# A decoder's first self-attention on one core: projections ahead of all stack loads, three split buffers, and weight loads moved into the main steps

## The reference, cut to what matters

```python
qkv = x @ w_in.T + b_in
q, k, v = jnp.split(qkv, 3, axis=-1)                    # 16 heads of 16 features
scores = jnp.einsum('bhqd,bhkd->bhqk', q * scale, k) + causal_bias
attn = jax.nn.softmax(scores, axis=-1)
out = jnp.einsum('bhqk,bhkd->bhqd', attn, v).transpose(0, 2, 1, 3).reshape(...) @ w_out.T + b_out
x = _layernorm(x + out)
```

## Time and profile before

| what | value |
|---|---|
| median of three runs | 2646.59 us (2644.69 to 2653.12) |
| the profiled execution's own time | 2647.83 us |
| its span, first to last instruction | 2646.0 us |
| mean granted TensorE clock | 0.918 of full speed |
| PE, DVE, ACT, POOL busy | 80%, 55%, 47%, 25% of the span |
| DMA moved | 139.78 MB, mean 53 GB/s |

### The profile page before, as it was taken

One profiled execution on the slowest core, in us unless ns is written; L12 is line 12 of the kernel. 1 busy time (PEld: TensorE's weight loads), 2 busy tenths in 40 slices (PEclk: granted clock), 3 DMA queues, 4 the chain that ended last, 5 costly groups with the idle time before them and its releaser, 6 DMA issues. The chain is left out here.

```text
span 2646.0 us, 32547 instructions
## 1 busy us (share of the span) xinstructions
PE 2120.5 (80%) x11571; PEld 1193.6 (45%) x11586; DVE 1460.5 (55%) x2643; ACT 1243.4 (47%) x2672; POOL 674.2 (25%) x750
## 2 busy tenths in 40 slices
PE   3688888888888689999999533989899756787786
PEld 1234344344342455565555412556566532444444
DVE  3545366366563276766667368476662233556555
ACT  1154544544535265555555173757522223374662
POOL 4610320220010100000000257464340231432222
PEclk7799999999999899999999756999999967898898
DMA  6422433432321100000000100000000254533311
GB/s 162 120 58 67 88 70 72 84 74 57 67 49 37 59 19 7 19 15 19 17 7 11 62 26 0 27 16 25 11 27 13 89 98 97 117 84 85 68 52 41
DMA packets 127859, 139.78 MB, mean 53 GB/s; under 512 B 35933, under 2 KB 102369, under 8 KB 127602
## 3 DMA queue, kind: packets, MB, share of 16 engines
q1 hardware_dynamic: 127698, 137.69, 22.5%
HBM read 99.16 MB, written 38.47 MB: 52 GB/s over the span
## 5 line engine op out<-in xcount | busy, mean ns | idle before, releaser
L512 ACT ACTIVATE pbuf_sb<-psB 128x512 f32<-128x512 f32 (+1 forms) x608 | 330.7, 573 | 323.2 <-PE psB L394 300.5
L679 DVE TENSOR_REDUCE negm_sb<-psA 128x1 f32<-128x768 f32 (+6 forms) x352 | 346.9, 1022 | 159.1 <-PE psA L382 156.6
L1036 ACT ACTIVATE pw_sb<-psA,nmx_sb 128x154 f32<-128x154 f32 x512 | 192.0, 387 | 194.4 <-DVE nmx_sb L1127 194.4
L391 PE MATMUL psB<-qst_sb,kst_sb 99*128 99x512 bf16 (+3 forms) x768 | 232.3, 332 | 42.9 <-ACT pbuf_sb L512 34.7
L380 PE MATMUL psA<-kst_sb,qst_sb 96*128 96x512 bf16 (+3 forms) x768 | 198.2, 337 | 28.5 <-DVE negm_sb L679 25.4
L1127 DVE TENSOR_REDUCE nmx_sb<-psA 128x4 f32<-128x616 f32 x128 | 102.3, 799 | 176.4 <-PE psA L904 176.4
L408 PE MATMUL psO<-pbuf_sb,V_sb 128*32 128x512 f32 (+3 forms) x1536 | 168.0, 510 | 8.7 <-ACT OT_sb L498 7.4
L2481 DVE TENSOR_REDUCE negm_sb<-psA 128x4 f32<-128x640 f32 x128 | 104.0, 812 | 126.8 <-PE psA L2153 126.7
L2308 ACT ACTIVATE pb_sb<-psB 128x512 f32<-128x512 f32 x160 | 92.2, 598 | 150.3 <-PE psB L2163 149.9
L391 PEld LDWEIGHTS psB<-qst_sb,kst_sb 99*128 99x128 bf16 x768 | 74.3, 98 | 179.7 <-ACT pbuf_sb L512 146.3
L1076 POOL TENSOR_SCALAR std_sb<-mv_sb 128x1 f32<-128x1 f32 x32 | 7.3, 228 | 503.4 <-DVE mv_sb L1154 503.4
(11 more groups left out here) (267 smaller groups left out, 4550.1 us busy)
## 6 DMA issues: line engine op xcount, KB each, us to landing
qst_sb<-parts_dram SPq DMA_DIRECT2D x192, 128.0 KB, 4.4
rden_sb<-dens_dram SPq DMA_DIRECT2D x128, 128.0 KB, 2.7
parts_dram<-parts_sb SPq DMA_DIRECT2D x32, 384.0 KB, 2.5
kst_sb<-parts_dram SPq DMA_DIRECT2D x96, 128.0 KB, 7.1
x_dram<-X_sb SPq DMA_DIRECT2D x64, 128.0 KB, 1.7
parts_dram<-partsb_sb SPq DMA_DIRECT2D x16, 384.0 KB, 2.8
xT_sb<-xT SPq DMA_DIRECT2D x4, 1024.0 KB, 5.4
X_sb<-x SPq DMA_DIRECT2D x4, 1024.0 KB, 5.3
```

The source lines that it names most:

```text
L391: last = nc.tensor.matmul(psB[:, k, at:at + hi - lo], kst[0:MAX_ROWS, gg % 3, h, i * P:(i + 1) * P], qst[0:MAX_ROWS, gg % 3, h, lo:hi], st ...
L512: nc.scalar.activation(pbuf[:, key % 2, heads[0]:heads[-1] + 1, lo:hi], psB[:, (nb.n - 1) % 2, 0:len(heads) * (hi - lo)] .rearrange("p (h ...
L679: nc.vector.tensor_reduce(out=negm[:, gg % 2, heads[0]:heads[-1] + 1, j], in_=psA[:, (na.n - 1) % 2, :].rearrange("p (h n) -> p h n", h=le ...
L1036: last = nc.scalar.activation(pw[:, m % 2, h, :], psA[:, m % 2, at:at + K], ACT.Exp, bias=nmx[:, m % 2, h:h + 1], accum_out=psx[:, m % 3, ...
```

## The change: what it does, and the diff

- **Prologue loads.** The bias of q and k is loaded first, with a semaphore of its own; PE waits for wqkv (and xT0) alone. The raw feed-forward weights are no longer loaded here.
- **Three buffers of `q32`.** ACT may run one unit further ahead of the split.
- **SP's order.** Store units 0 to 4, stack 0, store units 5 to 7, then the main steps: xT0 of batch 1 and stack 1 at k = 0, `first_weights` (output projection, raw weights, `ones_dram`) at k = 1, stack 2 at k = 3, `late_weights` (13 DMAs) at k = 31.
- **Raw weights** are loaded into the room of `wk_x0` and `wv_x0`, which hold cross-attention weights later; so those are loaded only once the quantised weights are made. DVE sums them at k = 9 and 10, PE adds up at k = 12, POOL quantises in six steps at k = 18, 20, ..., 28. ACT no longer waits for them at k = 10.
- **Constants.** POOL fills only the columns of V that need ones, and the rows of `kst` one stack at a time: two before its eight `rest_of`, the third after.
- **Fourth stage.** Two bias rows (128 KB each when broadcast) are loaded there and not in the first stage.

```diff
-    q32 = sb("q32", [P, 2, 512], F32, first_stage)
+    q32 = sb("q32", [P, 3, 512], F32, first_stage)
-    w_raw = OT[:, 0:4, :].rearrange("p (i a) n -> p i (a n)", i=2)
+    ones = rden[:, 0:P]
+    w_raw1, w_raw2 = wk_x0[:, :, :], wv_x0[:, :, :].rearrange("p c n -> p (c n)")
+    W_AT = 12
 # SP
+            sp.dma_start(bqk_a0[:, :], t["L0_attn_b_inC"][:, 0:4]).then_inc(bqk_loaded, 16)
             sp.dma_start(wqkv[:, :, :], feature_rows(t["L0_attn_w_inT"])).then_inc(first_loaded, 16)
             sp.dma_start(xT0[:, :, :], ...).then_inc(xt_loaded, 16)
+            sp.dma_start(bv_a0[:, :], ...).then_inc(bv_loaded, 16)
...
-            for u in range(4):
+            for u in range(5):
                 store_parts(0, u)
             parts_landed(4)
             load_stack(0)
-            load_stack(1)
-            for u in range(4, 8):
+            for u in range(5, 8):
                 store_parts(0, u)
-            parts_landed(8)
-            load_stack(2)
+            def first_weights():
+                sp.wait_ge(wo_zeroed, 1)
+                ...                                     # wo_a0 (4 DMAs), bo_a0
+                sp.dma_start(w_raw1, feature_rows(t["L0_ffn_w1T"])).then_inc(raw_loaded, 16)
+                sp.dma_start(w_raw2..., feature_rows(t["L0_ffn_w2T"])).then_inc(raw_loaded, 16)
+                sp.wait_ge(consts_made, 3)
+                sp.dma_start(ones_dram, kst[QK_ROWS:QK_ROWS + 1, 0, 0, :]).then_inc(ones_stored, 16)
+            def late_weights():
+                sp.wait_ge(quantised, 2)
+                ...                                     # wk_x0, wv_x0, wq_x0 and ten small ones
             for k in range(LAST + 1):
                 if k < UNITS and kk == 0 and b + 1 < B:
                     ...                                 # xT0 of the next batch
+                if k == 0:
+                    load_stack(1)
+                if k == 1:
+                    first_weights()
+                if k == 3:
+                    parts_landed(8)
+                    load_stack(2)
+                if k == 31:
+                    late_weights()
                 if k >= 1 and qk_unit(k - 1):
                     store_parts(*qk_unit(k - 1))
 # PE
-            pe.wait_ge(first_loaded, 16 * 3)
+            pe.wait_ge(first_loaded, 16)
...
-            pe.wait_ge(summed, 2)
             pe.wait_ge(consts_made, 1)
+                if k == W_AT:
+                    pe.wait_ge(summed, 2)
+                    a = slot_a()
+                    nc.tensor.matmul(psA[:, a, 0:2], ones[:, :], asum[:, :], start=True, stop=True).then_inc(a_full, 1)
 # ACT, store_qk
-                if at >= 2:
-                    act.wait_ge(split_made, at - 1)
+                if at >= 3:
+                    act.wait_ge(split_made, at - 2)
-                    if s == 0:
-                        act.wait_ge(quantised, 2)
 # POOL
-            nc.gpsimd.memset(V[:, :, :, :], 1.0).then_inc(v_cleared, 1)
+            ...                                         # two fills of 256 elements a partition each
-            nc.gpsimd.memset(kst[QK_ROWS:MAX_ROWS, :, :, :], 1.0).then_inc(consts_made, 1)
-            for u in range(8):
-                rest_of(u)
+            for i in range(3):
+                nc.gpsimd.memset(kst[QK_ROWS:MAX_ROWS, i, :, :], 1.0).then_inc(consts_made, 1)
+                pool.wait_ge(consts_made, i + 1)
+                if i == 1:
+                    for u in range(8):
+                        rest_of(u)
+                if 18 <= k < 30 and k % 2 == 0:
+                    quantise((k - 18) // 2)
 # DVE
-            dve.wait_ge(first_loaded, 16 * 3)
+            dve.wait_ge(bqk_loaded, 16)
+                    if k in (W_AT - 3, W_AT - 2):
+                        sum_weights(k - W_AT + 3)
+                    if k == W_AT:
+                        weight_scales()
 # fourth stage, SP
             sp.dma_start(wkv_x1[:, :, :], feature_rows(t["L1_xattn_Wkv"])).then_inc(kv_loaded, 16)
+            sp.dma_start(bv_x1[:, :], ...).then_inc(kv_loaded, 16)
+            sp.dma_start(bo_x1[:, :], ...).then_inc(bo_loaded, 16)
```

More of the change, by code:

```diff
@@ L213, in a_slots @@
     def a_slots(k):
-        return NT + 1 + sum((len(first_units(query_tile(i))) + (i % 8 == 7) if i < UNITS else 0)
+        return NT + (k > W_AT) + sum((len(first_units(query_tile(i))) + (i % 8 == 7) if i < UNITS else 0)
                             + bool(v_unit(i)) + bool(out_unit(i)) for i in range(k))
@@ L287, in _ @@
[L287 to L295, removed]
@@ L419, in _ @@
                 project_v(0, j)
-            pe.wait_ge(summed, 2)
             pe.wait_ge(consts_made, 1)
-            k = slot_a()
-            nc.tensor.matmul(psA[:, k, 0:2], ones[:, :], asum[:, :], start=True, stop=True).then_inc(a_full, 1)
             exps_at = {}
@@ L483, in store_qk @@
                 act.wait_ge(b_full, nb.up())
-                if at >= 2:
-                    act.wait_ge(split_made, at - 1)
-                nc.scalar.activation(q32[:, at % 2, :], psB[:, (nb.n - 1) % 2, :], ACT.Identity,
+                if at >= 3:
+                    act.wait_ge(split_made, at - 2)
+                nc.scalar.activation(q32[:, at % 3, :], psB[:, (nb.n - 1) % 2, :], ACT.Identity,
                                      bias=bqk_a0[:, 2 * qk + c:2 * qk + c + 1],
@@ L491, in store_qk @@
                     act.wait_ge(parts_stored[at % 3], 16 * (at // 3))
-                nc.scalar.activation(parts[:, at % 3, 0, :], q32[:, at % 2, :], ACT.Copy).then_inc(p1_made, 1)
+                nc.scalar.activation(parts[:, at % 3, 0, :], q32[:, at % 3, :], ACT.Copy).then_inc(p1_made, 1)
             def copy_out(gg, c):
@@ L536, in rest_of @@
                 pool.wait_ge(p1_made, at + 1)
-                nc.gpsimd.tensor_tensor(q32[:, at % 2, :], q32[:, at % 2, :], parts[:, at % 3, 0, :],
+                nc.gpsimd.tensor_tensor(q32[:, at % 3, :], q32[:, at % 3, :], parts[:, at % 3, 0, :],
                                         ALU.subtract).then_inc(rest_made, 1)
@@ L543, in split_qk @@
                 rest_of(at)
-                link(nc.gpsimd.tensor_copy(parts[:, at % 3, 1, :], q32[:, at % 2, :]))
-                nc.gpsimd.tensor_tensor(parts[:, at % 3, 2, :], q32[:, at % 2, :], parts[:, at % 3, 1, :],
+                link(nc.gpsimd.tensor_copy(parts[:, at % 3, 1, :], q32[:, at % 3, :]))
+                nc.gpsimd.tensor_tensor(parts[:, at % 3, 2, :], q32[:, at % 3, :], parts[:, at % 3, 1, :],
                                         ALU.subtract).then_inc(split_made, 1)
@@ L580, in _, with quantise @@
[L580 to L586, removed]
+            def quantise(step):
+                i = step // 3
+                raw = (w_raw1, w_raw2)[i]
+                if i == 0:
+                    raw = raw.rearrange("p c n -> p (c n)")
+                if step == 0:
+                    pool.wait_ge(m1_ready, 1)
+                if step % 3 == 0:
+                    link(nc.gpsimd.tensor_scalar(raw, raw, rs1[:, i:i + 1], ROUND, ALU.mult, ALU.add))
+                if step % 3 == 1:
+                    link(nc.gpsimd.tensor_scalar(raw, raw, ROUND, 1.0, ALU.subtract, ALU.min))
+                if step % 3 == 2:
+                    nc.gpsimd.tensor_scalar((w1q, w2q)[i][:, :, :].rearrange("p c n -> p (c n)"), raw, -1.0, None,
+                                            ALU.max).then_inc(quantised, 1)
+                    pool.wait_ge(quantised, i + 1)
@@ L605, in split_first @@
             def split_first(u):
-                link(nc.vector.tensor_copy(parts[:, u % 3, 1, :], q32[:, u % 2, :]))
-                nc.vector.tensor_tensor(parts[:, u % 3, 2, :], q32[:, u % 2, :], parts[:, u % 3, 1, :],
+                link(nc.vector.tensor_copy(parts[:, u % 3, 1, :], q32[:, u % 3, :]))
+                nc.vector.tensor_tensor(parts[:, u % 3, 2, :], q32[:, u % 3, :], parts[:, u % 3, 1, :],
                                         ALU.subtract).then_inc(split_made, 1)
@@ L662, in _, with sum_weights, weight_scales @@
             dve.wait_ge(v_cleared, 1)
+            dve.wait_ge(bv_loaded, 16)
             for j in range(NT):
                 take_v(0, j)
[L666 to L670, removed]
+            def sum_weights(i):
+                dve.wait_ge(raw_loaded, 32)
+                raw = (w_raw1.rearrange("p c n -> p (c n)"), w_raw2)[i]
+                nc.vector.tensor_reduce(out=asum[:, i:i + 1], in_=raw, axis=AX_X, op=ALU.add,
+                                        apply_absolute_value=True).then_inc(summed, 1)
+            def weight_scales():
+                dve.wait_ge(a_full, na.up())
+                nc.vector.tensor_scalar(m1[:, :], psA[:, (na.n - 1) % 2, 0:2], 1.0 / (FH * P * D), EPS, ALU.mult,
+                                        ALU.max).then_inc(a_free, 1)
+                dve.wait_ge(a_free, na.n)
+                nc.vector.reciprocal(rs1[:, :], m1[:, :]).then_inc(m1_ready, 1)
             for k in range(LAST + 1):
```

54 lines of the change are left out of this document (29 added, 25 removed).

## The result

The changed kernel takes 2625.03 us (median of six runs, 2622.55 to 2632.55) against 2646.36 for the kernel before (2643.95 to 2655.72): ratio 0.9914, 95% interval [0.9893, 0.9935]. It is 21 us faster, 17 to 28 by the interval. The forecast was 2612 with a range of 2602 to 2626: the direction holds, the range holds by 1 us, and the size does not quite, 35 us against 21 to 28. The profiled execution has a span of 2622.5 us, 23.5 less than that of the kernel before.

The account below looks back on a forecast made before the run. Two holes at the start, both from SP's queue order, were taken as the bound. -40.8 + 0.9 + 0.4 + 4.2 = -35.3 from the profiled 2647.8 gives 2612.5; median 2611, rounded up to 2612; range 2602 to 2626.

Parts of the forecast that it names:

- The two holes: TensorE idle 27 us up to 61.06 and 15.1 us before batch 1, from SP's order; step 10 gains 40.8 us.
- The cadence and its cause: Prologue split: three parts buffers set 6.1 us per three units, 2.03 for one; unit 7's rest ends at 30.6.
- The wait before step 10: PE waits 1.4 us for group 0's maxima, at the end of SP's queue; step 10 starts at 83.3.
- the terms of the queue: SP's transfers from 43.9: 2.6 + 11.3 + 6.1 + 11.3, then 3.4 us; claimed drained at about 80.5.
- the prediction's own sign of being wrong: SP blocking in issuing for over 5 us between 44 and 65 would make the prediction wrong.
- The rival of the transfers: Queue before step 10: 2.5 MB at 139 instead of 407 GB/s, step 10 12 us later; 2624, chance 0.16.
- The sums: DVE's raw-weight sums, 2.2 to 2.3 us each: first costs 0.9, second nothing; matmul and scales 0.4.
- POOL's quantising: Steps 18 to 28: a 7.11 us operation holds DVE's cast L618 in step 23, 5.1 late, costing 4.2 us.
- one hold: Step 23: POOL holds only the cast L618; 4.2 us, the forecast case, chance 0.38.
- the two-hold case: Step 23: POOL holds both L618 and L619; 9.6 us, 5.4 more than forecast, 2617, chance 0.20.
- Late weights: SP at step 31: late loads cost nothing, slack 19 us; rival that they hold SP: 2650 or more, chance 0.02.
- Fourth stage: Two DMAs, 0.9 us of issue, before SP's wait for POOL's fill of wo: 0, or 0.9 if not hidden.

Follow-up runs that it names:

- q32_two: Changed kernel with two buffers of q32 instead of three, in the prologue and the main steps; ratio 0.9919 to the kernel before.
- stacks_first: Changed kernel with SP again storing units 0 to 3, loading stacks 0 and 1, then storing units 4 to 7; 2640.06 us, ratio 0.9966.
- xt_late: Changed kernel with xT0 of batch 1 issued in step 3, behind stack 1, raw weights and stack 2; 2641.95 us, ratio 0.9986.
- gate_both: Changed kernel with GpSimd's two last quantising steps waiting until the maxima of group 2 are split; 2620.9 us, ratio 0.9882.
- best: Changed kernel with two last quantising steps after maxima split, third fill after unit split, raw-weight sums in steps 12 and 13; 2607.76 us, ratio 0.9856.
- before_again: The kernel before, unedited, profiled a second time; one run, 2659.57 us.

## Why the prediction was right in its range and off in its size

- **The two holes.** Right in cause and sum. The main steps were to start at 43.0 and did at 44.78; the value projections took 8.6 us where I had taken 7.8. Step 10 was to come at 83.3 and came at 83.1 in one profile and 85.5 in the other. Each hole was put back alone: 19.9 and 21.4 us.
- **The cadence and its cause.** The rest of unit 7 was forecast to end at 30.6; its cast started at 31.72, held for 3.81 us as expected. The cadence was credited to the parts buffers, and q32_two confirms that the third q32 buffer adds nothing.
- **The wait before step 10.** 1.4 us forecast, 0.62 and 3.88 measured. The 1.4 was partly luck: the terms of the queue, from 43.9, add up to 78.6 and not to the 80.5 that the prediction went on with, and from 78.6 no wait comes out. The longer waits go with an SP that is stuck longer in the issue of `ones_dram`, 4.75 us in the first profile and 6.27 in the second; over 5 us was the prediction's own sign of being wrong. Why the same program differs so from one execution to the next stays open. The rival of the transfers falls in size (12 us), not in kind. The low clock behind this wait had no term in the sum. Together they lengthen the distance of groups 0 to 1 by 3.4 us in the first pair of profiles and 4.6 in the second.
- **The sums.** Costed at 0.9 + 0.4, with the second sum at nothing, "I let it fit (2.2 if it does not)". It did fit: in stacks_first and xt_late both sums stand in steps 9 and 10 and the distance is at most 0.5 us over that of the kernel before.
- **POOL's quantising, the step that failed.** The collision with step 23 was foreseen in place and kind; its size was taken as one hold, 4.2 us, because the cast had the nearer row, though the two-hold case was worked out as 9.6 us. It measured 8.6 between averages, 9.8 us more busy time of VectorE in the first pair. What decides the second hold is that GpSimd had its next operation ready: at 171.48 it begins, 0.03 us before the subtraction. The rule quoted in the prediction from the Trainium skill ("SBUF — State Buffer", "Who interferes with whom") had both waits in it. The trace agrees that the cast waited for the whole operation under way, that the subtraction with two SBUF inputs was held by the next one, and that the reductions were not: six of them beside GpSimd's operations from 157.4 on took 6.35 us, as before. It differs in one thing, and the measurement decides: the subtraction did not wait out the whole 5.36 us but 3.5 of them, in all eight profiles with both holds (the profile's spans of GpSimd are rough).
- **Late weights.** Hidden, as forecast: SP issued the thirteen DMAs from 206.7 to 216.9 and the maxima followed at 223.6. **Fourth stage:** 63.8 us from its first load to its first maxima before, 63.3 after; no cost.
- **The rest of the difference.** Forecast -35.3 in the profiled execution; measured -23.5 in the first pair and -36.4 in the second, so no single pair can be split to the microsecond. In the first pair 11.8 are missing. By its marks 6.9 of them lie in step 23 (11.1 less the 4.2 forecast; 4.4 by the averages), 2.1 between groups 0 and 1 (3.4 less 1.3), 2.3 between groups 2 and 3, and 3.3 in the last stretch; 1.9 come back between group 3 and the last, and 0.8 were gained early over the forecast. The last stretch is the clock of two executions; between groups 2 and 3 gate_both and best have the 47.0 us of before_again, so that is no cost of the change either. At the last group's maxima, ahead of that stretch, the gain is 26.8 and 30.0 us. Of the 5 to 9 us that are missing there the holds explain 4.4 and the wait with its clock 2 to 3.
- **Luck.** The range held by 1 us, and its upper end came from the transfer rival and not from the second hold or from the clock.

## What to carry to other kernels

Where one engine issues all transfers, its order is a schedule: ask of each entry what is waiting behind it; here, at the first group's maxima, one misplaced 1 MB load cost 21 us and 24 small ones 20. Work moved from a prologue into a pipeline must be checked against what the other engines do at that moment, not on average: long GpSimd operations in a row can hold each VectorE cast or two-operand SBUF operation of a chain in turn, so put them behind a semaphore that says that VectorE's short chain is through. Read the cost from marks that recur in the program, and profile the same kernel twice before explaining a difference of a few microseconds. When an experiment comes out as its theory says, look whether the other runs bear the theory out too: moving the sums brought the expected 3 us, and two runs that had not moved them had the same 3 us.

## What the runs showed of the hardware

Two instructions of 0.21 and 0.28 us lasted 6.69 and 3.75 us beside GpSimd's, while six reductions from PSUM beside its operations took 6.35 us, as without them. A GpSimd fill of only 3 partitions (3.51 us) held a cast of 128 partitions to its end. An issue on SP's queue can itself last: 4.75 us for a 2 KB store with stack 1 and the raw weights issued before it, and 6.27 in another execution of the same program; issues of 4.1 to 4.8 us went with a wait of TensorE of 0.4 to 1.3 us some 25 us later, and issues of 5.3 to 6.4 us with 3.1 to 3.9. With each of these seven waits the granted clock in the first five us of step 10 was 0.50 to 0.66, and 1.00 in the six profiles without one. The granted clock of one stretch differed between two executions of one program (0.76 and 0.85) and moved its length by 4 us.
